# A Mamba mixer with an expert feed-forward: the causal mask inside the rows' contraction, bf16 parts on VectorE, and narrow running-sum products

## The reference, cut to what matters

```python
a = dtc * A                                  # per token and head (8 heads)
cum = jnp.cumsum(a, axis=2)                  # running sum inside a chunk of 128 tokens
diff = cumT[..., :, None] - cumT[..., None, :]
mask = jnp.tril(jnp.ones((CHUNK, CHUNK), bool))
decay = jnp.where(mask, jnp.exp(jnp.where(mask, diff, 0.0)), 0.0)
scores = jnp.einsum('bclhg,bcshg->bchls', Cc, Bc) * decay * dtT[:, :, :, None, :]
Y_intra = jnp.einsum('bchls,bcshp->bclhp', scores, Xc)
y = (Y_intra + Y_inter + D_skip[:, None] * Xc).reshape(B, L, D_INNER)
```

## Time and profile before

| | |
|---|---|
| median of 3 runs | 2614.18 us (2614.05 to 2617.98) |
| profiled execution, its own time | 2616.56 us |
| its span, first to last instruction | 2614.8 us |
| mean granted TensorE clock | 0.991 of full speed |
| TensorE matmuls busy | 2521.9 us, 96% |
| VectorE busy | 2120.7 us, 81% |
| GpSimd busy | 2168.8 us, 83% |
| ScalarE busy | 1824.3 us, 70% |
| one group in the loop | 78.95 us, of which TensorE is busy 77.87 us |

### The profile page before, as it was taken

One profiled execution on the slowest core, in us unless ns is written; L12 is line 12 of the kernel. 1 busy time (PEld: TensorE's weight loads), 2 busy tenths in 40 slices (PEclk: granted clock), 3 DMA queues, 4 the chain that ended last, 5 costly groups with the idle time before them and its releaser, 6 DMA issues. The chain is left out here.

```text
span 2614.8 us, 58427 instructions
## 1 busy us (share of the span) xinstructions
PE 2521.9 (96%) x18552; PEld 2004.5 (77%) x18616; DVE 2120.7 (81%) x5397; ACT 1824.3 (70%) x3745; POOL 2168.8 (83%) x3130
## 2 busy tenths in 40 slices
PE   5899999999999999999999999999999999999987
PEld 4677877877877878777778777778777778778766
DVE  5688888878888878888878888878888888888877
ACT  4577777677777677777777777767777767776754
POOL 4488888888888888888888888888888888888875
PEclk8999999999999999999999999999999999999999
DMA  4000000000000000000000000000000000000000
GB/s 144 9 9 14 6 12 8 12 12 12 4 8 12 12 12 12 4 8 12 12 12 12 4 8 12 12 12 12 4 8 12 12 12 5 11 8 12 9 5 9
DMA packets 28861, 34.33 MB, mean 13 GB/s; under 512 B 2704, under 2 KB 27280, under 8 KB 28240
## 3 DMA queue, kind: packets, MB, share of 16 engines
q1 hardware_dynamic: 28816, 33.77, 4.1%
HBM read 25.37 MB, written 8.39 MB: 13 GB/s over the span
## 5 line engine op out<-in xcount | busy, mean ns | idle before, releaser
L1221 DVE SCALAR_TENSOR_TENSOR acc<-bank,cw,acc 128x253 f32<-128x253 f32 x1920 | 770.3, 472 | 102.3 <-ACT acc L858 102.3
L1618 PE MATMUL bank<-hT,w_in 128*128 128x256 f32 x2560 | 618.4, 385 | 13.8 <-DVE acc L1221 11.3
L1618 PEld LDWEIGHTS bank<-hT,w_in 128*128 128x128 f32 x2560 | 480.5, 192 | 129.7 <-issue 38.5
L645 POOL TENSOR_TENSOR Em<-ee 128x1024 f32<-128x1024 f32 x256 | 490.4, 1926 | 11.1 <-DVE rden L1357 6.3
L1377 DVE SCALAR_TENSOR_TENSOR Em<-Em,p 128x1024 f32<-128x1024 f32 x256 | 354.0, 1413 | 85.3 <-POOL Em L645 85.3
L660 POOL TENSOR_TENSOR W<-W,Em 128x1024 f32<-128x1024 f32 x124 | 295.0, 2379 | 51.4 <-ACT Em L993 43.5
L858 ACT ACTIVATE acc<-bank,cb,cw 128x253 f32<-128x253 f32 x640 | 324.0, 559 | 0.0
L993 ACT ACTIVATE Em<-Em,rden 128x1024 f32<-128x1024 f32 x256 | 289.9, 1145 | 47.4 <-DVE Em L1387 45.6
L1387 DVE TENSOR_TENSOR Em<-Em,products 128x1024 f32<-128x1024 f32 x248 | 297.3, 1210 | 0.0
L1810 PE MATMUL bank<-h2T,w_up 128*128 128x256 f32 x1024 | 244.8, 382 | 2.1 <-ACT hid L971 1.4
L1844 PE MATMUL bank<-w_ue,WT 128*128 128x256 f32 x1024 | 234.1, 382 | 0.2 <-ACT WT L1003 0.2
(11 more groups left out here) (210 smaller groups left out, 5013.1 us busy)
## 6 DMA issues: line engine op xcount, KB each, us to landing
x_in<-x_dram SPq DMA_DIRECT2D x32, 256.0 KB, 2.7
x_res<-x_dram SPq DMA_DIRECT2D x32, 256.0 KB, 2.7
out_dram<-f SPq DMA_DIRECT2D x32, 256.0 KB, 2.2
w_in<-in_wT_dram SPq DMA_DIRECT2D x1, 1544.0 KB, 8.8
w_in<-in_wT_dram SPq DMA_DIRECT2D x1, 1024.0 KB, 5.3
w_up<-upT_dram SPq DMA_DIRECT2D x1, 1024.0 KB, 13.2
w_de<-down_eT_dram SPq DMA_DIRECT2D x1, 1024.0 KB, 15.2
w_down<-downT_dram SPq DMA_DIRECT2D x1, 1024.0 KB, 17.5
```

The lines of the kernel that those rows point to most:

```text
L645: nc.gpsimd.tensor_tensor(Em[:, k], bc(ee[:, k, 0:XD], 2, KEYS), bc(ee[:, k, XD:XD + KEYS], 1, XD), ALU.mult).then_inc(E_done.sem, 1)
L1221: ins = V.scalar_tensor_tensor(acc[:, r, a, TAPS - 1:], ps[:, a * TOK + k:(a + 1) * TOK - TAPS + 1 + k], cw[:, t, k:k + 1], acc[:, r, a, T ...
L1618: last = mm(ring[j % 2][:, a * TOK:(a + 1) * TOK], w_in[:, k, at:at + P], hT[:, k, :], start=k == 0, stop=k == DK - 1)
```

## The change

1. **The mask moves into the contraction.** `cum_parts` becomes 128 x 2 x 128, the second index for the lower and upper 64 output partitions. Partitions 0 to 47 hold the three parts (16 columns each, no padding), partitions 48 to 111 the causal mask of those 64 output rows, written once at the start. The weights `picks` (16 sets of 64 columns) hold the three ones of a head and, under them, a 64 x 64 identity. One product with 112 contracted partitions and 64 output partitions makes a masked half of a head. A chunk takes sixteen of them; the mask products are gone.
2. **VectorE makes the parts**, in five instructions on 48 partitions, between `mixer_stats(n)` and `mixer_conv(g, 9)`. GpSimd's six are gone.
3. **The first chunk's `sL` products come in front of its skip products.** The second chunk keeps the old order.
4. **The running sums and the total** are made in four products of 32 output partitions each instead of one of 128; the transposed sums keep their single product.

```diff
-        da = sb("da", [P, 4, 2 * CH * HEADS])
+        da = sb("da", [P, P])
-        cum_parts = sb("cum_parts", [P, P], BF16)
+        cum_parts = sb("cum_parts", [P, 2, P], BF16)
...
+            for half in range(2):
+                nc.gpsimd.affine_select(out=cum_parts[:, half], in_=cum_parts[:, half], compare_op=ALU.is_ge,
+                                       fill=MASKED, base=PARTS - half * HALF, pattern=[[1, P]],
+                                       channel_multiplier=-1).then_inc(own_pool, own.one())
...
+            nc.gpsimd.tensor_tensor(picks[:], bc(pick[:], 2, HALF), bc(ident[:, PARTS:PARTS + HALF], 1, CH * HEADS),
+                                    ALU.add).then_inc(own_pool, own.one())
...
                 if a:
                     mixer_cum(g)
-                    mixer_parts(g)
...
+            def mixer_parts(g):
+
+                dve.wait_ge(cum_sb.sem, cum_sb.at(g))
+                if later(g):
+                    dve.wait_ge(rows_ps.sem, rows_ps.at(g - 1, 2 * CH - 1))
+                V.tensor_copy(cum_parts[0:PARTS, 0], cumT[0:PARTS]).then_inc(own_dve, own.one())
+                dve.wait_ge(own_dve, own.n)
+                V.scalar_tensor_tensor(cum_rest[0:PARTS], cum_parts[0:PARTS, 0], minus_a[0:PARTS, 0:1], cumT[0:PARTS],
+                                       ALU.mult, ALU.add).then_inc(own_dve, own.one())
+                dve.wait_ge(own_dve, own.n)
+                V.tensor_copy(cum_parts[0:PARTS, 0], cum_rest[0:PARTS]).then_inc(own_dve, own.one())
+                dve.wait_ge(own_dve, own.n)
+                V.scalar_tensor_tensor(cum_parts[0:PARTS, 1], cum_parts[0:PARTS, 0], minus_b[0:PARTS, 0:1],
+                                       cum_rest[0:PARTS], ALU.mult, ALU.add).then_inc(parts_done.sem, 1)
+                V.scalar_tensor_tensor(cum_parts[0:PARTS, 0], cum_parts[0:PARTS, 0], minus_b[0:PARTS, 0:1],
+                                       cum_rest[0:PARTS], ALU.mult, ALU.add).then_inc(parts_done.sem, 1)
...
                 if n is not None:
                     mixer_stats(n)
+                if g is not None:
+                    mixer_parts(g)
                 if a:
                     mixer_conv(g, 9)
...
-                mm(yb[:, 0:n], tri[:], da[:, 0, 0:n], start=True, stop=True)
-                mm(yb[:, n:2 * n], ones[:], da[:, 0, 0:n], start=True, stop=True)
-                mm(yb[:, P:2 * P], da[:].rearrange("p a b -> p (a b)"), tri[:], start=True, stop=True)\
+                for t in range(0, P, 32):
+                    mm(yb[t:t + 32, 0:n], tri[:, t:t + 32], da[:, 0:n], start=True, stop=True)
+                for t in range(0, P, 32):
+                    mm(yb[t:t + 32, n:2 * n], ones[:, t:t + 32], da[:, 0:n], start=True, stop=True)
+                mm(yb[:, P:2 * P], da[:], tri[:], start=True, stop=True)\
                     .then_inc(cum_ps.sem, 1)
...
-                    mm(pairb[q][:], ident_b[:], mask_b[:].rearrange("p h t -> p (h t)"), start=True, stop=False)
                     for i in range(4):
-                        h = 4 * q + i
-                        k = c * HEADS + h
-                        last = mm(pairb[q][:, i * P:(i + 1) * P], pick[:, k:k + 1].to_broadcast([P, P]), cum_parts[:],
-                                  start=False, stop=i == 3)
+                        for half in range(2):
+                            last = mm(pairb[q][half * HALF:(half + 1) * HALF, i * P:(i + 1) * P],
+                                      picks[0:PARTS + HALF, c * HEADS + 4 * q + i, :],
+                                      cum_parts[0:PARTS + HALF, half, :], start=True, stop=True)
                     last.then_inc(rows_ps.sem, 1)
```

More of the change, by code:

```diff
@@ L24 @@
 HALF = 64
+PARTS = 48
 CH = 2
@@ L352, in _ @@
             nc.gpsimd.memset(ident[:], 0.0).then_inc(own_pool, own.one())
-            nc.gpsimd.memset(mask_b[:], 0.0).then_inc(own_pool, own.one())
+            nc.gpsimd.memset(cum_parts[:], 0.0).then_inc(own_pool, own.one())
             nc.gpsimd.memset(edges[:], 0.0).then_inc(own_pool, own.one())
@@ L368, in _ @@
                 .then_inc(own_pool, own.one())
-            nc.gpsimd.affine_select(out=mask_b[:], in_=mask_b[:], compare_op=ALU.is_ge, fill=MASKED,
-                                   base=0, pattern=[[0, 4], [1, P]], channel_multiplier=-1)\
-                .then_inc(own_pool, own.one())
+            for half in range(2):
+                nc.gpsimd.affine_select(out=cum_parts[:, half], in_=cum_parts[:, half], compare_op=ALU.is_ge,
+                                       fill=MASKED, base=PARTS - half * HALF, pattern=[[1, P]],
+                                       channel_multiplier=-1).then_inc(own_pool, own.one())
             nc.gpsimd.affine_select(out=ident[:], in_=ident[:], compare_op=ALU.not_equal, fill=1.0,
@@ L374, in _ @@
                 .then_inc(own_pool, own.one())
-            for first, minus in ((64, minus_a), (96, minus_b)):
+            for first, minus in ((CH * HEADS, minus_a), (2 * CH * HEADS, minus_b)):
                 nc.gpsimd.affine_select(out=minus[:], in_=minus[:], compare_op=ALU.is_ge, fill=0.0,
@@ L516, in mixer_cum @@
                 nc.gpsimd.tensor_scalar(ncum[:], cum[:, 0], -1.0, None, ALU.mult).then_inc(cum_diff.sem, 1)
-            def mixer_parts(g):
-                pool.wait_ge(cum_sb.sem, cum_sb.at(g))
-                if later(g):
-                    pool.wait_ge(rows_ps.sem, rows_ps.at(g - 1, 2 * CH - 1))
-                pool.sem_inc(arrived_pool, 1)
-                nc.gpsimd.tensor_copy(cum_parts[:], cumT[:]).then_inc(own_pool, own.one())
-                pool.wait_ge(own_pool, own.n)
-                nc.gpsimd.tensor_scalar(cum_rest[:], cum_parts[:], minus_a[:, 0:1], None, ALU.mult)\
-                    .then_inc(own_pool, own.one())
-                pool.wait_ge(own_pool, own.n)
-                nc.gpsimd.tensor_tensor(cum_rest[:], cum_rest[:], cumT[:], ALU.add).then_inc(own_pool, own.one())
-                pool.wait_ge(own_pool, own.n)
-                nc.gpsimd.tensor_copy(cum_parts[:], cum_rest[:]).then_inc(own_pool, own.one())
-                pool.wait_ge(own_pool, own.n)
-                nc.gpsimd.tensor_scalar(cumT[:], cum_parts[:], minus_b[:, 0:1], None, ALU.mult)\
-                    .then_inc(own_pool, own.one())
-                pool.wait_ge(own_pool, own.n)
-                nc.gpsimd.tensor_tensor(cum_parts[:], cum_rest[:], cumT[:], ALU.add).then_inc(parts_done.sem, 1)
             def mixer_keep(g):
@@ L1644, in mixer_rows @@
                 if c == 0:
[L1645 removed]
+                    pe.wait_ge(parts_done.sem, parts_done.at(g, 1))
                 for q in range(2):
@@ L1730, in mixer_Yn @@
                     pe.wait_ge(cum_sb.sem, cum_sb.at(g))
-                pe.wait_ge(skips, INNER // P)
-                for i in range(INNER // P):
-                    mm(yb[:, i * P:(i + 1) * P], xbcT[:, i, c * P:(c + 1) * P],
-                       skip[:, 2 * i:2 * i + 2, :].rearrange("p h d -> p (h d)"), start=i == 0, stop=False)
+                if c:
+                    pe.wait_ge(skips, INNER // P)
+                    for i in range(INNER // P):
+                        mm(yb[:, i * P:(i + 1) * P], xbcT[:, i, c * P:(c + 1) * P],
+                           skip[:, 2 * i:2 * i + 2, :].rearrange("p h d -> p (h d)"), start=i == 0, stop=False)
                 pe.wait_ge(Xdt_done.sem, Xdt_done.at(g, c))
@@ L1740, in mixer_Yn @@
                         last = mm(yb[t:t + HALF, h * HD:(h + 1) * HD], sL[:, h, t:t + HALF],
-                                  Xdt[:, h * HD:(h + 1) * HD], start=False, stop=h == HEADS - 1)
+                                  Xdt[:, h * HD:(h + 1) * HD], start=c == 0 and h == 0,
+                                  stop=c > 0 and h == HEADS - 1)
+                if c == 0:
+                    pe.wait_ge(skips, INNER // P)
+                    for i in range(INNER // P):
+                        last = mm(yb[:, i * P:(i + 1) * P], xbcT[:, i, c * P:(c + 1) * P],
+                                  skip[:, 2 * i:2 * i + 2, :].rearrange("p h d -> p (h d)"), start=False,
+                                  stop=i == INNER // P - 1)
                 last.then_inc(Yn_ps.sem, 1)
```

14 lines of the change are left out of this document (6 added, 8 removed).

## The result

| | before | after |
|---|---|---|
| device time, median (runs) | 2615.33 us (2614.05 to 2617.98, 4 runs) | 2585.66 us (2584.86 to 2586.19, 4 runs) |
| span of the profiled execution | 2614.8 us | 2584.5 us |
| one group of the loop, groups 3 to 30 | 78.955 us | 77.811 us |

The ratio of the times is 0.9885 with an interval of 0.9868 to 0.9902. The kernel became 1.2% faster. The forecast was 2574 us in a range of 2565 to 2602, so direction and range held. The time lies at the upper end of the narrower band of 2566 to 2586. The span fell by 30.3 us instead of 40.3, so 10 us were missing.

A forecast was written before the change was run, and what follows sets the result against it. TensorE's own stream plus 0.52 us per group waiting for parts bound the kernel; 14.6 + 0.8 + 0.6 + 5.1 + 21.4 - 1.5 - 0.7 sum to 40.3 us, from 2616.56 to 2576.3, median 2574 us, range 2565 to 2602.

The forecast's parts named there:

- The wait on the parts: TensorE's 0.52 us per group waiting for GpSimd's last part goes; VectorE's five instructions take 1.45 us, `prod` still waits.
- The halves: Row products: sixteen of 64 output partitions stream as eight overlapping pairs, 0.46 us for a chunk.
- serial halves: Rival at the row products: the halves don't overlap in bf16, a chunk costs 0.88 us, 2600 to 2602; chance 0.12.
- exposed weight loads: Rival at the row products: the halves' weight loads aren't hidden, a chunk costs 1.68 us, 2649 us; chance 0.05.
- Pauses: On TensorE, each change of product width costs a pause of 0.09 to 0.11 us.
- the order of Yn: Second chunk, rows following the state, then `sL`, then skip products: gain 0.67 us per group, 21.4 us in all.
- the running sums: Narrow products for TensorE's running sums: 0.65 us against 0.67 before; gain taken as 0.0, between -0.10 and +0.10.
- First chunk: 30 x 0.17: Rows of the first chunk, between wide neighbours: gain 0.17 us in each of 30 groups, 5.1 us.
- I charge 0.05 us per group: At the transposes, ScalarE's `head` ends at 1080.77 just as TensorE wants it; loss 0.05 us per group, 1.5 us.
- the prediction's own signs of being wrong: Row records 0.055 us apart; `prod` without a wait; new TensorE wait on `head`, `Xw` or B; running sums over 0.77 us.
- another wait takes over: Rival: VectorE's parts cost 2.2 to 2.4 us or `head` comes later; 0.3 to 0.7 us per group lost; chance 0.13.
- GpSimd's Xw moves by some 0.7 too: On GpSimd, `Xw` comes some 0.7 us earlier, since the root before it waited for an expert product now starting early.

The follow-up runs named there:

- `ee` by a copy: The changed kernel with the search's exponential replaced by a copy, so ScalarE loads no tables around it; output not the reference's; 2577.35 us.
- the late table: The changed kernel with `picks` built on GpSimd behind the first group's loads instead of in front of everything; 2584.12 us.
- wide sums: The changed kernel with the running sums and the total in one product of 128 output partitions each, as before; 2584.46 us.

## Why the prediction was right, and where it was short

- **The wait on the parts: right.** It is gone, VectorE's five steps took 1.41 us (1.45), `prod` still waited. The kernel before with the move alone gains 0.45 us per group; the changed kernel without it loses 0.80, a seventh step on GpSimd included.
- **The halves: right.** 0.45 us for a chunk (0.46). The kernel with the lower half twice shows why: 0.056 us for each product in one half, with nothing to pay for the other. The rivals on serial halves and on exposed weight loads fell; so did, for these products, the sentence of the Trainium skill's "TensorE: Matmul & The Clock Gate", The mechanism, that loads overlap running products only if their row group differs. The same section of the Trainium skill also lets a load run ahead into a background buffer for weights, which the prediction passed over.
- **Pauses, the order of Yn, the running sums: right.** 0.64 (0.67) and 0.00 (0.0). At full width the second chunk pays two pauses of 0.10 more. Here the trace agrees with the rule of the Trainium skill's "TensorEngine Tiling (Array Packing)", Key Properties, that a change of mode drains the engine.
- **"First chunk: 30 x 0.17": the products gained it, the period didn't.** The rows of the first chunk shrank by 0.22 us, but with the parts moved the transposes and the state start where they start with the old rows, 11.35 and 20.81. The move is worth 0.45, the second chunk 0.70, the first chunk 0.00; together that is the group's 1.14, but for rounding (1.31 forecast). The next two points say what holds these stations.
- **"I charge 0.05 us per group" for the next wait: too small, by 0.12.** The prediction let `head` end at 1080.77 and the transposes start in the same moment. Both traces show 0.23 us between them: 1080.97 + 0.25 to 1081.46 in the earlier trace rows, 1071.36 to 1071.59 after. That row was in hand, and the gap in it was read as nothing. Without a wait the stretch from the expert sum takes 3.56 us (lower half twice, `ee` by a copy) and the kernel before took 3.72, so TensorE already waited 0.16 there. And I took GpSimd for what held `head`, since the row named it; what holds it is ScalarE's own queue, which has no idle time from `ee` to `head`. Doubling the lower half, going to full width, and taking the table loads away (0.33 us earlier) show it three times. A new wait on `head` was one of the prediction's own signs of being wrong, and so was one on `Xw`; the period is 77.81 us, not 77.6 to 77.7. The rival "another wait takes over" came true at 0.25 us per group, a little under its 0.3 to 0.7, inside its 2583 to 2595 us.
- **"GpSimd's Xw moves by some 0.7 too": wrong, 0.13 per group.** GpSimd's chain to `Xw` does not count from the parts but from `rden`, for which the first expert product waits; that wait stands in the code and I passed over it. VectorE's `rden` hangs on `ee`, which ScalarE makes, and comes no earlier relative to the transposes. In the kernel before, `rden` was there at 1080.88 and `Em` started at 1081.02: GpSimd had 0.14 us to gain, not 0.7, before it would come upon `rden`. So GpSimd's freed time became a wait of 2.98 us, and `Xw` is on the path. The copy in place of `ee` shows that it takes over as soon as `head` is early, and doubling the lower half that it holds the state at 20.72.
- Together with 0.03 less at Yn and 0.10 more elsewhere this is 0.17 us per group, 28 x 0.17 = 4.8 (4.7 by the spans) of the 10 missing. The spans give the rest (the forecast's terms sorted by place, gains in us):

| place | forecast | measured |
|---|---|---|
| up to the first running sum | 0 | -1.97 |
| group 0 | 0.6 + 0.67 = 1.27 | 0.79 |
| group 1 | 0.67 | -2.08 |
| group 2 | 1.19 | 1.02 |
| groups 3 to 30 | 28 x 1.31 = 36.7 | 32.03 |
| last group and end | 0.49 | 0.58 |

- **The start: not in the sum, 2.0 us.** `picks` is a new table, 1.90 us on GpSimd in front of the first load that TensorE waits for. The prediction priced the loop and left the start at zero. What is left of it at the start of group 1 is 0.7 to 0.8 us, as the late table shows. TensorE's first product, at 10.73 us before, comes at 12.72:

```profile
5.27 1.90 POOL L386 TENSOR_TENSOR picks<-pick,ident 128x1024 bf16<-128x1024 bf16 x1
...
12.72 1.09 PE L1587 MATMUL bank<-ident,hn 128*128 128x128 f32 x4 [12.72 <-ACT hn L781]
```

- **Group 0: 0.5 us.** Its wait for the parts was to turn into a wait for the transposes; it grew from 3.3 to 4.0 us instead, for VectorE's last part, and the transposes' wait stayed (2.54 us before, 2.74 after).
- **Group 1: 2.7 us, the clock's; why it was low is open.** The gain there was to be 0.67 us, but the distance to group 2 grew by 2.08. The same 11 us in both kernels (us, busy us and records, granted clock, DMA share, GB/s), after and then before:

```profile
134.00:145.00 11.00, 9.81 (x60) 0.69 0.01 2
```

```profile
134.00:145.00 11.00, 10.54 (x113) 1.00 0.01 2
```

TensorE had waited 2.70 us in front of the transposes, 2.39 before the change. But the length of the wait doesn't decide. Four kernels with the same instructions in that place but for the sums wait 2.7 us there each, and had a granted clock of 0.88 (changed kernel), 0.89 (wide sums, late table), 0.96 (wide sums) and 1.00 (late table) from 135 to 160 us; group 1 took 83.23, 83.21, 81.94 and 80.52 us. At 1.00 it is 0.63 us shorter than the 81.15 before, close to the forecast's 0.67. So the 2.7 us are the clock's, and neither the new products nor the wait bring the low clock by themselves. The times of one kernel differ with the clock too: with wide sums 2581.43 us at a mean of 0.992 of full speed, 2587.59 at 0.990. What brings the low clock in one execution and not in another was not tried further.

The 4.7, 2.0, 0.5 and 2.7 us are the 10 missing, but for 0.1 at the other two places. Half of them were lost in the loop, half in front of it.

## What to carry to other kernels

Where a wait is taken off the path, list for each later station every wait of its producer in the code, and follow them to their own anchor; "moves along" holds only if that anchor moves. A time saved in front of a station that waits for another engine is worth nothing until that wait is gone. Read the hand-over between engines as a term of its own, from the row where the station already waits. And price what a change adds in front of the loop: it is paid once, here with 2.0 us up to the first running sum, of which 0.7 to 0.8 were left a group later.

## What the runs showed of the hardware

- Products for the lower and the upper 64 output partitions run side by side, whether they alternate or come four and four (0.56 against 0.60 us for sixteen in front of a wide product, 0.45 for both between narrow ones; four of one half in front don't hold back the other); in one half they follow each other at 0.056 us for 128 bf16 columns. With the lower half twice, a product of one half even starts ahead of one of the other half that stands before it (1086.15 and 1086.20).
- The weight loads of such products, 0.11 us each, cost nothing beside them: sixteen products with sixteen loads take 0.45 us.
- A contraction over 112 rows costs no more than one over 128: eight full-width products take 0.45 us, 0.056 each, as the head products of the earlier trace rows do.
- A 1024-wide fp32 product on GpSimd of 1.94 us held a 64-wide operation of VectorE that started beside it until the end: 2.24 instead of 0.53 us for the four. The masking of such a product took 2.05 and 2.58 us beside GpSimd's wide products, and 1.28 us where GpSimd had a two-column operation beside it; that one took 1.32 us, the next of its size 0.22.
- The same instructions took 80.52 to 83.23 us in the second group of four profiled executions, at granted clocks of 1.00 to 0.88.
